# Two masks ahead of the branch: DVE works on the first tile before it reads the path flag

## The reference, cut to what matters

```
def _gat_conv(x, src, dst, W, a_src, a_dst, b, n_nodes):
    h = x @ W.T
    alpha_s = h @ a_src
    alpha_d = h @ a_dst
    e = _leaky(alpha_s[src] + alpha_d[dst], NEG_SLOPE_ATT)
    m = jax.ops.segment_max(e, dst, num_segments=n_nodes)
    ex = jnp.exp(e - m[dst])
    z = jax.ops.segment_sum(ex, dst, num_segments=n_nodes)
    alpha = ex / z[dst]
    msg = h[src] * alpha[:, None]
    out = jax.ops.segment_sum(msg, dst, num_segments=n_nodes) + b
    return out
```

## Time and profile before

| | |
|---|---|
| median of the runs | 857.66 us (857.34 to 858.0) |
| span of the profiled execution (first to last instruction) | 855.0 us |
| PE busy | 740.5 us, 87% |
| DVE busy | 629.5 us, 74% |
| ACT busy | 478.1 us, 56% |
| gat1, by the barrier before and the first matmul of it | 494.3, 497.08 us |
| gat2, the same | 652.6, 655.36 us |

### The profile page before, as it was taken

How to read it: one execution, slowest core, us unless ns; L and a number is a source line. 1 busy time by engine, 2 the same in 40 slices (tenths; PEclk the granted TensorE clock), 3 DMA queues, 4 the chain that set the end, 5 groups by cost and what they waited for, 6 DMA issues and landing times. The chain is left out here.

```text
span 855.0 us, 21138 instructions
## 1 busy us (share of the span) xinstructions
PE 740.5 (87%) x8244; PEld 671.7 (79%) x8244; DVE 629.5 (74%) x1696; ACT 478.1 (56%) x911; POOL 4.3 (0%) x14
## 2 busy tenths in 40 slices
PE   6888888887997998999997679998863999986998
PEld 6665556557996998999997668897763988875997
DVE  7899999986355545433444789998988999987832
ACT  2698889881004123122224578887765988875500
POOL 1000000000000000000000000000000000000000
PEclk9799999998996999999999579999965999999899
DMA  4000000004990000000002100000001399875901
GB/s 137 12 12 13 12 4 2 1 2 152 416 409 7 2 2 1 2 2 2 13 13 93 32 2 17 17 17 2 2 1 33 81 183 186 178 154 146 202 25 34
DMA packets 98734, 56.01 MB, mean 66 GB/s; under 512 B 91160, under 2 KB 93130, under 8 KB 98504
## 3 DMA queue, kind: packets, MB, share of 16 engines
q1 hardware_dynamic: 98292, 53.78, 23.2%
q10 hardware_dynamic: 340, 0.84, 0.3%
HBM read 9.16 MB, written 24.97 MB: 40 GB/s over the span
## 5 line engine op out<-in xcount | busy, mean ns | idle before, releaser
L624 PE MATMUL banks<-y_sb,adjacency 128*128 128x192 f16 (+1 forms) x1875 | 167.3, 250 | 6.0 <-DVE y_sb L661 5.2
L624 PEld LDWEIGHTS banks<-y_sb,adjacency 128*128 128x128 f16 x1875 | 162.8, 99 | 7.0 <-DVE y_sb L661 5.3
L462 PEld LDWEIGHTS counts<-hot_code,hot_row 128*128 128x128 f16 x1568 | 90.7, 99 | 66.1 <-DVE hot_code L345 41.4
L462 PE MATMUL counts<-hot_code,hot_row 128*128 128x100 f16 (+3 forms) x1568 | 122.3, 217 | 23.2 <-DVE hot_code L345 17.6
L1755 PE MATMUL banks<-loose,y_sb 128*128 128x194 f16 x540 | 100.6, 250 | 0.0
L345 DVE TENSOR_TENSOR hot_code<-codes_iota,unpacked 128x600 f16<-128x600 f16 x196 | 96.8, 554 | 0.0
L565 ACT ACTIVATE adjacency<-counts 128x800 f16<-128x800 f32 x98 | 81.7, 833 | 21.5 <-PE counts L462 21.5
L1754 PE MATMUL banks<-x_sb,gat_masks 128*128 128x194 f16 x420 | 79.3, 251 | 16.2 <-DVE gat_masks L1677 8.2
L1754 PE MATMUL banks<-x_sb,y_sb 128*128 128x194 f16 x400 | 74.4, 248 | 13.9 <-DVE h_sb L1677 9.9
L1725 ACT ACTIVATE gat_masks<-y_sb,node_scalars 128x640 bf16<-128x640 f32 x84 | 67.9, 825 | 21.9 <-PE banks L1755 16.7
L1754 PE MATMUL banks<-x_sb,h_sb 128*128 128x194 f16 x430 | 75.8, 247 | 0.8
(11 more groups left out here) (244 smaller groups left out, 1342.0 us busy)
## 6 DMA issues: line engine op xcount, KB each, us to landing
kept_adj<-adjacency SPq DMA_DIRECT2D x5, 4000.0 KB, 32.1
y_sb<-a_dst_rows SPq DMA_DIRECT2D x10, 320.0 KB, 3.7
window_keys<-edge_keys SPq DMA_DIRECT2D x188, 5.0 KB
residual<-h_sb SPq DMA_DIRECT2D x5, 240.0 KB, 2.0
kept_x<-x_sb SPq DMA_DIRECT2D x1, 1200.0 KB, 4.5
loose<-residual SPq DMA_DIRECT2D x5, 240.0 KB, 3.7
x_sb<-kept_x SPq DMA_DIRECT2D x5, 240.0 KB, 4.7
x_sb<-in_x SPq DMA_DIRECT2D x4, 240.0 KB
```

The lines of the kernel that those rows point to most:

```text
L462: last = nc.tensor.matmul(counts[:, 2 * (p % HELD) + i, start:end], hot_row[:, q % 2, b * QUAD + w, :], hot_codes(q % 2, b)[:, w, start - ...
L624: return nc.tensor.matmul(k.ps[:, j % G, 0:cols], k.ADJ[:, i, j * P:(j + 1) * P], y[:, i, 0:cols], start=i == 0, stop=i == NT - 1)
```

## The change

Two things are done. `over` and `under` become functions of the whole `attend`, and DVE issues over(0) and under(0) ahead of its flag read; the loop of `small_vector` leaves both out. The loop then begins with over(1), then over(2), under(1), and so on as before. And the semaphores over_ready and under_ready move behind the fourteen shared ones; two unused names take their places, so each `attend` holds two semaphores more.

```
-        t = semaphores(nc, k, name, "chain exact_max over_ready under_ready used bank_done first_out both_out z_ready sum_ready "
-                       "h_written row_0 row_1 exact_larger step_ready vectors tiles_turned measured")
+        t = semaphores(nc, k, name, "chain exact_max exact_turned exact_shifted used bank_done first_out both_out z_ready sum_ready "
+                       "h_written row_0 row_1 exact_larger step_ready over_ready under_ready vectors tiles_turned measured")
...
-            over(0)
             for x in range(steps):
...
                 if drains:
-                    under(x)
+                    under(dve, x)
...
                 if x + 1 < steps:
-                    over(x + 1)
-                if not drains:
-                    under(x)
+                    over(dve, x + 1)
+                if not drains and x:
+                    under(dve, x)
...
         @block.vector
         def _(dve):
+            over(dve, 0)
+            under(dve, 0)
             wide = dve.value_load(k.wide[0:1, 0:1], min_val=0, max_val=1)
             with dve.If(wide):
                 dve.wait_ge(t.step_ready, UNBRANCHED)
```

More of the change, by code:

```diff
@@ L1666, in small_sync, with over, under @@
             sp.wait_ge(t.row_1, 16)
-        def small_vector(dve):
[L1669 to L1677, removed]
+        def over(dve, x):
+            dve.wait_ge(t.step_ready, x + 1)
+            dve.tensor_tensor(over_of(x), step_of(x), counts_of(x), ALU.min).then_inc(t.over_ready, 1)
+        def under(dve, x):
+            dve.wait_ge(t.over_ready, x + 1)
+            if under_slots[x][1]:
+                dve.wait_ge(t.used, under_slots[x][1])
+            dve.tensor_tensor(under_of(x), counts_of(x), over_of(x), ALU.subtract).then_inc(t.under_ready, 1)
+        def small_vector(dve):
             def add(ch, q):
```

## The result

Over 21 executions each, the kernel before takes 857.74 us (median) and the changed one 859.1. The ratio is 1.0013, with a 95% interval of 1.0007 to 1.0019, so the change costs 1.1 us (0.6 to 1.6). The predicted time was 858.9. One execution of the kernel before took 3968 us, and one of a later experiment (only over(0) ahead) 1823 us; such executions are left out of the ratios.

The account below looks back on a forecast made before the run. It took PE's steady stream, begun by under(2) and passed through a ring of engine waits, to bound each stage; 0.61 + 0.61 = 1.2 us raises the span from 855.0 to 856.2, with 2.66 outside 858.9 us, range 857.0 to 860.8.

Parts of the forecast that it names:

- What bounds the entry: At both attention stages' entries, PE's stream is unbroken only from step 2, so under(2) matters, not under(0).
- The instants: DVE's entry: over(0) 0.36 us earlier, under(0) 0.65 earlier, flag read 1.42 later in gat1, under(2) 0.61 later per stage.
- its bounds: DVE's moved flag read, taken as 1.22 us: a longer load adds 0.24 per stage; a shorter branch cuts 0.61 to 0.1.
- That the read waits behind under(0): On DVE's queue at the entry, the flag read starts only once under(0) is let go; this decides the sign.
- The second rival: On DVE, the read overtakes under(0), making under(2) 0.25 us earlier; 857.2 us, chance 0.13.
- The semaphores: Names only move; POOL's longer clear beside the entry costs nothing, or some tens of ns without cover.
- The sum: Both stages' entries together: 0.61 + 0.61 = 1.2 us slower, giving 858.9 us; likeliest case, chance 0.50.
- rival 1: PE's clock rises later, 2.0 us lost in gat2; 860.1 us, or 861.7 if in both stages; chance 0.25.
- Absorption, the third rival: DVE's slack later in the stage takes the delay in; 857.7 us, chance 0.12.

Follow-up runs that it names:

- read first: Changed kernel with DVE's flag load moved ahead of over(0) and under(0), the branch staying behind them; ratio 1.0001 to the kernel before.
- the better order: Changed kernel with DVE's flag load first, then over(0), under(0), over(1), branch, over(2), under(1), under(2), over(3); ratio 1.0001 to the kernel before.
- doubled and fourfold loads: Changed kernel with DVE's flag loaded twice or four times; ratios to the kernel before 1.0039 (+3.3 us) and 1.0083 (+7.1 us).
- fillings: Unread PE matmuls ahead of its flag read and between its first pairs; 854.23 us on the changed kernel, 854.2 on the kernel before, 854.93 on the better order.
- long fillings: PE filled with unread matmuls from the end of the preparation on; 855.43 us on the changed kernel, 855.25 on the kernel before, 854.37 on the better order.

## Why the prediction was right, point by point

**What bounds the entry: right.** The stream from the third pair on sets the stage's length. The first pair, 0.64 us earlier, brought nothing in the changed kernel, in "read first" and in the better order.

**The instants: right within 0.03 us.** Behind step 0: over(0) at 0.86 (predicted 0.87), the load at 1.40 (1.43), over(1) at 2.62 (2.65), under(2) at 4.23 (4.26); in gat2 the delay of under(2) was 0.58 (0.61). The read in its new place took 1.22 us, the value taken, and neither of its bounds: the load took 310 ns against the 553 of the earlier one.

**That the read waits behind under(0): right, and shown.** The doubled and fourfold loads move with it, and "read first" puts the load back beside ACT. The second rival is dead: the load, which carries no wait of its own, does not pass an instruction of its engine that still waits. The load stands until that wait is over, but not until the instruction is done: it began 0.01 us behind under(0)'s start.

**The semaphores: right,** shown by that part alone; the longer clear on POOL that was allowed for didn't show either.

**The sum: right in size, and that in part by luck.** 1.2 us was predicted and 1.1 (0.6 to 1.6) measured. The 0.61 per stage counted the delay in full, on the ground that the rise moves with the stream. The formula gives the delay itself 0.3 us per stage, 0.6 in all; the other 0.5 is the rise, and it didn't move with the stream. In gat1 it came 0.58 later and made the stage's +0.60 look as assumed, but the semaphores alone had it 0.56 later with no delay at all. In gat2 it did as in rival 1 (+3.4, stage +1.96; rival 1 said 2.0).

The 2.6 us of the two stages there are more than the median's 1.1, so other executions must have lost less. How many have the long low stretch in gat2 isn't known. Each execution's mean clock is on record, but it is too coarse for this: what it does show is the low stretches ahead of gat1. The changed kernel's executions with a mean clock of 0.934 or more have a median of 858.65 us (16), the others 859.63 (5); for the kernel before, timed beside the experiments, it is 857.38 (47) and 858.36 (27). The difference is 1.27 us both times, so a different share of such executions isn't the cause.

**Rival 1: a part of the result, with a wrong condition.** It was to decide as soon as PE's idle time between steps 0 and 2 grows. With over(0) alone that idle time is as before (0.32 us twice) and gat2's low stretch is 37.5 us all the same; with the read first it grows to 1.2 us and the low stretch stays at 34.1. What the longer stretch goes with is a late third pair. The fourfold read, 7.1 us against 5.0 one to one, is where it shows largest.

**Absorption, the third rival: wrong** at this side. No part of a delay was absorbed. On the other side, with PE early, some was.

**Where an expectation failed:** the better order, meant to gain 0.5 to 1.0 us, gained none that can be seen; in its profile the half of 0.53 was met by a rise 0.5 us later. The fourfold read cost 7.1 us where 5.0 was expected. The fillings' differences failed as told above, and the long fillings, expected at 853.9 us or less, came out at 854.37 to 855.43. The best kernels run are those with the filling: 854.2 us on the kernel before, 0.37% faster than it, and the changed order neither adds nor takes anything measurable there.

## What to carry to other kernels

Before moving work ahead of a flag read, ask whether that work waits. Here what stood behind the wait on DVE's queue waited too, the register load included, and it lost the cover it had. Load the flag first, put the waiting work behind it, and branch last; then the load is hidden and the work is early (here that only took the loss away, ratio 1.0001). And ask which of the early results starts the next engine's unbroken stream: here it was the third, and the first, 0.64 us earlier, brought nothing. Where that engine starts at the low clock, look at the clock's rise before looking at the order: a rise 3 us earlier was worth 3 us in all, and no order of masks tried here a measurable amount.

## What the runs showed of the hardware

- A load of a flag into a register, its register work and the branch cost DVE 0.70 us, and the first instruction behind the branch another 0.5; together 1.22 and 1.17 us in the two stages before, 1.22 in the changed kernel. A further load makes over(1) 0.61 us later (2.62, 3.23 and 4.46 behind step 0 with one, two and four).
- A register load without a wait doesn't pass a waiting vector instruction ahead of it (load at 1.40 behind step 0 in its place behind two waits, 0.01 in its place ahead of them).
- The time at which the clock rises is not a property of the kernel alone: with no change at the entry it moved by 0.56 us in gat1 (semaphores alone). A third pair 0.47 us or more later went with a low stretch of 37.5 us in gat2 instead of 34.1.
- Under the low clock a later start of PE's stream and a later rise each cost half of their size, within 0.07 us over sixteen stages.
- The rise can stay away in spite of a busy PE: PE was busy, mostly with matmuls of an identity, in 3.69 of 4.00 us at 490 to 494, 0.49 of the next 1.00 and all of 495 to 499, and the clock stood at 0.50 throughout; it rose at 499.84.
